# A graph network's layer passes: the transform of the preceding tile moved between two parts of a tile's sum

## What is computed

```
h = relu(layernorm(x))
for l in range(3):
    xr  = einsum('nd,rde->rne', h, W_rel[l])     # 8 relation types: h times 8 matrices
    msg = xr[edge_type, src]                     # one row of 256 per edge
    agg = segment_sum(msg, dst)                  # summed per receiving node
    h   = relu(agg + h @ W_root[l] + bias[l])
x = x + h                                        # and then the attention layer
```

## Time and profile before

| | us |
|---|---|
| median of three runs | 4475.43 |
| the profiled execution | 4462.39 |
| its span | 4460.7 |
| TensorE matmul busy | 3494.5 (78%) |
| GpSimd busy | 3085.8 (69%) |
| ScalarE busy | 1934.7 (43%) |
| VectorE busy | 1835.2 (41%) |

### The profile page before, as it was taken

One profiled execution on the slowest core, in us unless ns is written; L12 is line 12 of the kernel. 1 busy time (PEld: TensorE's weight loads), 2 busy tenths in 40 slices (PEclk: granted clock), 3 DMA queues, 4 the chain that ended last, 5 costly groups with the idle time before them and its releaser, 6 DMA issues.

```text
span 4460.7 us, 54591 instructions
## 1 busy us (share of the span) xinstructions
PE 3494.5 (78%) x12674; PEld 2415.4 (54%) x12674; DVE 1835.2 (41%) x5354; ACT 1934.7 (43%) x5102; POOL 3085.8 (69%) x3322
## 2 busy tenths in 40 slices
PE   8999888888887888888887666566665777777777
PEld 3446565555554555555554444444443666666666
DVE  4444444444442222222222111112112777777776
ACT  2334454444453545454544343434342444444444
POOL 1034777777775777777775777777776777777775
PEclk9998999999998999999998777887886888888888
DMA  6545666666664445444444444444443444444443
GB/s 207 202 173 204 206 224 213 216 212 211 212 225 150 162 152 162 153 162 152 162 153 133 117 118 117 119 117 119 117 118 100 117 120 119 119 118 120 118 120 91
DMA packets 240903, 683.98 MB, mean 153 GB/s; under 512 B 60408, under 2 KB 112212, under 8 KB 215892
## 3 DMA queue, kind: packets, MB, share of 16 engines
q0 software_dynamic: 153360, 421.67, 33.0%
q10 hardware_dynamic: 57240, 186.43, 11.3%
q1 hardware_dynamic: 29996, 72.34, 4.5%
HBM read 504.62 MB, written 175.58 MB: 152 GB/s over the span
## 4 chain that ended last, share of the span: by engine, by line
POOL 65%; issue 21%; PE 10%; DMA 2%; DVE 1%; SPq 0%; ACT 0%; ACTq 0%; DVEq 0%; POOLq 0%
POOL ring L581 65%; PE bank L1503 8%; DMA ring<-table,code 1%; PE sum_ps L1590 1%; PE sum_ps L1713 0%; PE turn_ps L1490 0%; DMA table<-stage 0%; DVE stage L759 0%; DMA bias_row<-in_L_gnn_bias_dram 0%; PE bank L1640 0%; PE bank L1669 0%; SPq L700 0%; DVE z L750 0%; DVE stats L739 0%; DMA h_table<-stage 0%
## 5 line engine op out<-in xcount | busy, mean ns | idle before, releaser
L581 POOL DMA_INDIRECT ring<-table,code x2376 | 2253.4, 948 | 822.1 <-issue 748.9
L1590 PE MATMUL sum_ps<-ring,masks 128*128 x5292 | 1424.5, 425 | 621.7 <-SPq L695 583.5
L1590 PEld LDWEIGHTS sum_ps<-ring,masks 128*128 128x128 f32 x5292 | 1080.5, 211 | 934.2 <-issue 779.2
L1503 PE MATMUL bank<-wide,xT 128*128 128x512 f32 (+1 forms) x2744 | 1158.3, 577 | 10.1 <-DMA bias_row<-in_L_gnn_bias_dram 4.5
L581 POOL DMA_INDIRECT ring<-h_table,code x792 | 760.1, 960 | 259.7 <-issue 259.7
L1503 PEld LDWEIGHTS bank<-wide,xT 128*128 128x128 f32 x2744 | 534.7, 197 | 586.5 <-issue 565.3
L1340 ACT ACTIVATE masks<-node_row,local 128x128 f32<-128x128 f32 x2646 | 788.0, 387 | 28.4 <-issue 13.7
L1247 ACT COPY stage<-bank 128x512 f32<-128x512 f32 x441 | 253.6, 583 | 833.8 <-PE bank L1503 833.7
L1713 PE MATMUL sum_ps<-ring,stage 128*128 x1764 | 484.2, 422 | 0.3 <-ACT stage L1440 0.3
L1238 ACT ACTIVATE xT<-turn_ps 128x256 f32<-128x256 f32 x196 | 75.5, 385 | 789.3 <-PE turn_ps L1490 786.1
L782 DVE SCALAR_TENSOR_TENSOR root<-bank,loops,root 128x256 f32<-128x256 f32 x686 | 330.8, 482 | 172.7 <-ACT stage L1247 131.8
(11 more groups left out here) (218 smaller groups left out, 2037.3 us busy)
## 6 DMA issues: line engine op xcount, KB each, us to landing
table<-stage ACTq DMA_DIRECT2D x96, 1024.0 KB, 4.6
back<-table ACTq DMA_DIRECT2D x49, 1024.0 KB, 5.4
table<-stage SPq DMA_DIRECT2D x48, 1024.0 KB, 4.1
ring<-table,code POOLq DMA_INDIRECT x2376, 2.8
ring<-h_table,code POOLq DMA_INDIRECT x792, 2.8
h_table<-stage ACTq DMA_DIRECT2D x49, 130.0 KB, 2.2
back<-h_table ACTq DMA_DIRECT2D x49, 130.0 KB
features<-xT SPq DMA_DIRECT2D x49, 128.0 KB, 4.0
```

Of the source, the lines that this page charges most:

```text
L581: pool.indirect_dma_start(slot(c % RING, width), None, table, bass.IndirectOffsetOnAxis(ap=code[:, c:c + 1], axis=0)).then_inc(landed[n % ...
L1503: last = nc.tensor.matmul(bank[q][:, 0:width], xT[:, b, k, :], weights[:, k, 512 * q:512 * q + width], start=(k == 0), stop=(k == K - 1))
L1590: last = nc.tensor.matmul(sum_ps[b][:, 0:D], masks[:, b, s, :], at_offset(slots[s]), start=(s == 0 and l > 0), stop=(s == SLOTS - 1))
```

## The change

In the passes l = 0 and 1 TensorE's order becomes, for every tile i from 1 to 48: pieces one and two of sum i, transform i-1, pieces three to five of sum i, turn i. At the end only transform 48 is left. VectorE's order becomes: first-loop steps of tile i (pass l = 0), evacuate i-1, add i. The special order at the end of a pass goes. `PARTED` is 1, so that the old order is used for no tile. The transform of tile 47 now also waits for the first-loop steps of tile 48. ScalarE, SyncE and GpSimd keep their programs.

```diff
@@ VectorE
-            def sum_up(l, i, j, b):
-                if l == 0:
+            def sum_up(l, i, j, b, loops_first=True):
+                if l == 0 and loops_first:
                     add_first_loops(i, j, b)
@@
                 sum_up(l, 0, 0, 0)
-                for j in range(0, PAIRS - 1):
-                    sum_up(l, 2 * j + 1, j, 1)
-                    next_table(l, 2 * j, j, 0)
-                    sum_up(l, 2 * j + 2, j + 1, 0)
-                    next_table(l, 2 * j + 1, j, 1)
-                sum_up(l, NT - 2, PAIRS - 1, 1)
-                next_table(l, NT - 3, PAIRS - 1, 0)
-                next_table(l, NT - 2, PAIRS - 1, 1)
-                sum_up(l, NT - 1, PAIRS, 0)
+                for i in range(1, NT):
+                    j, b = divmod(i, 2)
+                    if i < PARTED:
+                        sum_up(l, i, j, b)
+                        next_table(l, i - 1, (i - 1) // 2, 1 - b)
+                    else:
+                        if l == 0:
+                            add_first_loops(i, j, b)
+                        next_table(l, i - 1, (i - 1) // 2, 1 - b)
+                        sum_up(l, i, j, b, loops_first=False)
                 next_table(l, NT - 1, PAIRS, 0)
@@ TensorE
-            def sum_tile(l, where, j, b):
+            def sum_tile(l, where, j, b, pieces=range(PIECES)):
                 slots, groups = where
                 use = l * USES[b] + j
-                if l == 0:
+                if l == 0 and pieces[0] == 0:
@@
-                for c in range(PIECES):
+                for c in pieces:
@@
-                if l == 0 and (not isinstance(i, int) or i < NT - 2):
+                if l == 0 and i < NT - 1:
@@
                 sum_tile(l, load_plan(pe, 0), 0, 0)
                 where = load_plan(pe, 1)
                 turn_sum(l, 0, 0)
...
-                where = next_table(l, NT - 4, PAIRS - 2, 1, NT - 2)
-                turn_sum(l, PAIRS - 1, 0)
-                sum_tile(l, where, PAIRS - 1, 1)
-                next_table(l, NT - 3, PAIRS - 1, 0)
-                turn_sum(l, PAIRS - 1, 1)
-                where = next_table(l, NT - 2, PAIRS - 1, 1, NT - 1)
-                sum_tile(l, where, PAIRS, 0)
-                turn_sum(l, PAIRS, 0)
+                for i in range(1, NT):
+                    j, b = divmod(i, 2)
+                    ahead = range(PIECES) if i < PARTED else range(2)
+                    sum_tile(l, where, j, b, ahead)
+                    upcoming = next_table(l, i - 1, (i - 1) // 2, 1 - b, i + 1 if i < NT - 1 else None)
+                    if i >= PARTED:
+                        sum_tile(l, where, j, b, range(2, PIECES))
+                    turn_sum(l, j, b)
+                    where = upcoming
                 next_table(l, NT - 1, PAIRS, 0)
```

More of the change, by code:

```diff
@@ L68, in gnn_program @@
     BATCH = 16
+    PARTED = 1
     assert SLOTS <= CH and HELD + 2 * GROUP <= RING and HALF <= P and NCH == CH <= COLS and 0 < FAR_PAD
```

## The result

| | before, us | changed, us |
|---|---|---|
| median of the timed runs | 4478.24 (4475.34 to 4480.01) | 4458.21 (4448.72 to 4461.14) |
| the profiled execution | 4462.39 | 4448.72 |
| its span | 4460.7 | 4447.0 |

The ratio is 0.9956, 95% interval 0.9944 to 0.9967: 20 us faster, 15 to 25. The median of before is now that of five runs; the forecast started from three of them, 4475.43. The profiled executions differ by 13.7 us. The two differences are not the same number; the profiled execution of before lies 16 us under its median, that of the changed kernel 9.5 us, and nothing in the traces says why.

The account below looks back on a forecast made before the run. GpSimd issuing gathers bounds the passes; TensorE's order sets the time only in the gaps between them. Gains of 17.3 - 0.6 - 0.8 = 15.9, say 16 us, off the median 4475.43 give 4459.4 us, range 4456 to 4464.

Parts of the forecast that it names:

- (d): Ends of passes one and two: transform 48 starts sooner, gains of 9.0 and 8.3 us taken, together 17.3.
- (e): Pass ends: tile 46 late, 0 to 3 us per pass, 0.3 taken; pass two's clock loss, 0 to 1.7, half taken.
- its gathers had landed: End of pass one: sum 47 ends at 1356.7 as in the old order, without a wait for gathers.
- (f): Gather stalls inside pass one, some 4 us: bound 4 us less or up to 0.6 a tile more; no change taken.
- (b): Each turn right behind its sum: VectorE's addition exposed, 0.72 us, paid from a pass-one margin of 2.8 us per tile.
- (c): VectorE evacuates tile i-1 before adding tile i: evacuation covered by some 1.5 us, pass one's first-loop steps by 0.4.
- 1 and 5 (half arrives): Pass ends lose part of the gain, 4468 us, or only pass two gains, 4467; chance 0.18 together.
- Rival 2: 1 MB transfers stall gathers by 0.6 us in each of pass one's 48 tiles: 29 us, 4488; chance 0.08.
- rival 3: Waits lower TensorE's clock until a tile takes 20.3 us or more: two passes lose 221 us, 4680; chance 0.03.

Follow-up runs that it names:

- n6: TensorE in the new order, VectorE in the old one, otherwise the changed kernel plus one register step: 4713.63 us against 4481.61 of before on the same chip.
- n1: The changed kernel with one register step more on each group count, on a slower chip: 0.9987 of before.
- p1: The same kernel as n1, on another chip of the slower kind: 0.9991 of before.

## Why the prediction was right, point by point

**The bound and the place.** 16 us were forecast from the ends of two passes, 4459.4; measured were 20 (15 to 25) and a median of 4458.21, and 14.4 us in the two gaps of the trace. The place is right. That the median fell within 1.2 us of the forecast is in part luck: the trace accounts for 14 of the 20 us, and the starting point of 4475.43 was 2.8 us below the median of five runs. The gap of pass two is right to a few tenths: 8.2 us less, 8.3 forecast. Its waits and starts came as worked out, transform 48 at 8.7 us after the last gather, 8.6 in the forecast's middle.

**The gap of pass one** shrank by 6.1 us instead of 9.0, outside the 8.5 to 9.6. Two terms of (d) and (e) were mis-sized. The first: "its gathers had landed". The chain of the changed kernel shows the gather that tile 47's last piece needs, and ScalarE's queue beside it:

```profile
1351.82 4.81 DMA ring<-table,code
...
1351.98 0.33 ACTq L1293 DMA_DIRECT2D table<-stage  x1
```

It landed 4.8 us after its issue; the store of a table now goes out 0.16 us after it. Before, no 1 MB transfer was issued within 1 us of this gather (1352.82), and it landed in 2.7; the next one there (1354.07) had a load of 1 MB issued 0.26 us behind it and took 5.5. So late landings stand beside 1 MB transfers in both traces, though no run separates the two. Sum 47 so ends 8.8 us before the last gather issues, not 11.1. The prediction named such coincidences in (f) as a matter of stalls in the middle and took them at nothing; it should have carried one of 2.3 us as a bound of the end, where it isn't absorbed. The second: the clock. The window behind that wait, and then the two gaps:

```profile
1358.50:1362.00 3.50, 3.41 (x9) 2.79 (x10) 2.87 (x7) 0.38 (x1) 2.58 (x4) 0.52 0.36 107
...
1366.80:1390.30 23.50, 18.71 (x58) 10.38 (x56) 10.09 (x21) 6.82 (x18) 0.96 (x2) 0.98 0.28 102
2380.90:2401.00 20.10, 15.61 (x51) 8.94 (x49) 8.35 (x18) 3.14 (x7) 0.97 (x2) 0.97 0.33 119
```

0.52 is the level of 1.2 GHz for nearly all of the 3.5 us. Ahead of it TensorE had waited 1.43 us, worked 1.1 and waited 0.57. Turn, root term and the first 8 slots took 6.3 us, 1.6 longer than at 2.4 GHz. The forecast had a loss of just this size, half taken, but in pass two, where the waits looked longer and 0.3 us came. The two terms make 3.9 us, of which 2.9 reached the gap: the forecast's last sum waits for the last gather, the real one comes too late to wait. (The 1373 that (d) takes for a landing "as in rows 8" would be 1374.2 by that row; for the same reason nothing hung on it.)

By the Trainium skill ("TensorE: Matmul & The Clock Gate", "Why this matters for your kernels") gaps between bursts bring the clock down; what the runs add is that a short burst between two short waits didn't prevent it in pass one, while in pass two of the same run the wait of 2.86 us with 1.1 of work and 0.57 behind it cost almost nothing.

**(b)** was right: 0.57 us ahead of each turn, 0.72 forecast. **(c)** was right: VectorE's last evacuating step ends 1.6 us after the transform, TensorE never waits for L794, and no turn waits over 0.7. The thin cover of 0.4 us held in every tile. In these rows of tile 48 the first-loop steps end at 1363.08, 1.8 us before transform 47, because the low clock held TensorE up:

```profile
1358.45 0.48 DVE L794 SCALAR_TENSOR_TENSOR bank<-back,loops,root 128x256 f32<-128x256 f32 x1
...
1362.60 0.48 DVE L794 SCALAR_TENSOR_TENSOR root<-back,loops,bank 128x256 f32<-128x256 f32 x1
...
1373.73 0.42 DVE L768 TENSOR_TENSOR root<-bank,root 128x256 f32<-128x256 f32 x1
```

That VectorE's order is a part of the change and not an ornament, n6 shows: without it the kernel is 232 us slower than before. **(b)**'s margin was smaller than forecast: 1.7 us of waits for gathers a tile are left in pass one, not 2.8. A tile at full clock takes TensorE what was forecast: from turn to turn 927.93 - 909.57 us, less a wait of 0.73, are 17.6 against 17.5. The forecast had no low clock in the middle of a pass, where the mean is 0.94; that this makes the missing 1 us a tile is likely and not shown. **(e)**, tile 46: its last piece starts 1366.82 - 1336.14 = 30.7 us before the last gather, 30.4 before. The lag is no greater than before. The sign that the prediction set for it, later than 31 us, was met by before already (1367.80 - 1337.39 = 30.4), so it could tell nothing. **(f)**: six waits on SyncE of 0.4 us or more in pass one as before, 3.1 us in all beyond the usual 0.30 against 3.6, and three new ones in pass two, 1.8 us. No change in pass one, as taken; pass two's gathers take 1.7 us longer, which the sum had at nothing.

**The rivals.** 1 and 5 (half arrives), 2 (collisions in each tile) and 3 (TensorE bound) didn't come on the result's chip. Rival 2's mechanism did, once, at the place where it costs. What the prediction held against rival 3, that a TensorE which has become the bound keeps its clock, is not borne out by n6: there TensorE is the bound of pass one, still waits 5.35 us in most tiles, and its granted clock is 0.87. The slower chips were in no rival: TensorE doesn't wait for gathers there, and the change is worth 0.1% or nothing.

## What to carry to other kernels

Where a steady producer sets the pace, look at the consumer's order only at the seams: count how many large steps stand behind the last arrival, and move those that don't need it ahead of it; here an exposed hand-over of 0.6 us per tile cost nothing, since the waits for the producer were longer. Moving work on one engine is half a change if another engine's program order still follows the old one. At a seam nothing absorbs a late landing or a lower clock, so a sum of steps there wants an allowance for each; here they took 2.3 and 1.6 us.

## What was not expected of the hardware

The same program took 4478 us on some chips and 5350 to 5378 on others; the part before the first gather took 372 to 375 us on both. On the slower kind TensorE has stretches like this one of n1, the changed kernel, in which single matmuls stand apart with waits that nothing in the profile ends:

```profile
538.92 0.38 PE L1592 MATMUL sum_ps<-ring,masks 128*128 x1 [0.64 <-issue]
541.71 0.38 PE L1592 MATMUL sum_ps<-ring,masks 128*128 x1 [2.42 <-issue]
544.51 2.79 PE L1592 MATMUL sum_ps<-ring,masks 128*128 x5 [2.42 <-issue]
```

Single instructions at full clock take the same on both (a gather 0.95 us, a transform of the changed kernel 7.7), and what lies between instructions grew; GpSimd, ScalarE and VectorE are busy 3079, 1927 and 1828 us on the slower chip of p1, 3084, 1921 and 1833 in the result's trace. The cause is open.
